# A semaphore for each buffer of turned blocks, two V tiles behind each of two score tiles, and three transposes on VectorE and through DRAM

## The reference

```python
h = film(rmsnorm(x, norm1_w), cond, film1_w, film1_b)   # x*(1+scale)+shift, scale and shift from cond
Q, K, V = h @ q_w + q_b, h @ k_w + k_b, h @ v_w + v_b
attn = softmax(einsum('bnd,bmd->bnm', Q, K) * D ** -0.5)
x = x + (einsum('bnm,bmd->bnd', attn, V) @ proj_w + proj_b)
h = film(rmsnorm(x, norm2_w), cond, film2_w, film2_b)
out = x + gelu(h @ mlp_w1 + mlp_b1) @ mlp_w2 + mlp_b2   # 256 -> 1024 -> 256
```

## Time and profile before

| | us |
|---|---|
| median of 3 runs | 234.42 (234.26 to 234.46) |
| profiled execution | 234.09 |
| its span | 232.2 |
| TensorE matmuls busy | 218.7 (94% of the span) |
| VectorE busy | 148.5 (64%) |
| ScalarE busy | 110.4 (48%) |
| GpSimd busy | 70.9 (31%) |

### The profile page before, as it was taken

How to read it: one execution, slowest core, us unless ns; L and a number is a source line. 1 busy time by engine, 2 the same in 40 slices (tenths; PEclk the granted TensorE clock), 3 DMA queues, 4 the chain that set the end, 5 groups by cost and what they waited for, 6 DMA issues and landing times.

```text
span 232.2 us, 3530 instructions
## 1 busy us (share of the span) xinstructions
PE 218.7 (94%) x1284; PEld 190.4 (82%) x1284; DVE 148.5 (64%) x288; ACT 110.4 (48%) x207; POOL 70.9 (31%) x102
## 2 busy tenths in 40 slices
PE   0998999999889999999999899999999999999994
PEld 0767988978768999998999799888888888888994
DVE  0599767669598998989989575143724372436223
ACT  3158654425333355333363881377437743744440
POOL 1575752002325512852543224321232123200000
PEclk9999999999999999999999999999999999999999
DMA  6994000054568968654556420000200020002002
GB/s 165 342 401 181 3 12 35 3 180 139 182 220 271 259 204 265 204 181 164 182 201 236 143 57 0 3 0 0 90 3 0 0 90 3 0 0 92 3 0 90
DMA packets 15713, 26.72 MB, mean 115 GB/s; under 512 B 1872, under 2 KB 10064, under 8 KB 15568
## 3 DMA queue, kind: packets, MB, share of 16 engines
q1 hardware_dynamic: 13392, 18.11, 24.9%
q10 hardware_dynamic: 2304, 8.39, 9.4%
HBM read 16.00 MB, written 10.49 MB: 114 GB/s over the span
## 4 chain that ended last, share of the span: by engine, by line
PE 78%; DVE 9%; DMA 7%; issue 2%; SPq 2%; ACT 1%; ACTq 0%; DVEq 0%
PE psum L711 36%; PE psum L785 16%; PE psum L836 8%; PE psum L828 5%; PE psum L834 5%; DMA raw<-in_film_wT_dram 3%; PE psum L729 3%; DMA crossing<-raw 2%; PE psum L703 2%; PE psum L723 2%; DVE hT L516 1%; DMA keys_first<-crossing 1%; ACT probsT L404 1%; PE psum L833 1%; SPq L190 1%
## 5 line engine op out<-in xcount | busy, mean ns | idle before, releaser
L658 DVE TENSOR_TENSOR G_all<-probs,G_all 128x512 fp32r<-128x512 f32 x32 | 22.4, 706 | 46.3 <-ACT G_all L453 46.3
L785 PEld LDWEIGHTS psum<-V_all,probsT 128*128 128x128 f32 x384 | 47.1, 189 | 5.4 <-DVE probsT L613 4.6
L785 PE MATMUL psum<-V_all,probsT 128*128 128x256 f32 x384 | 48.3, 283 | 2.7 <-DVE probsT L613 2.6
L711 PE MATMUL psum<-hT,w 128*128 128x512 f32 x192 | 49.1, 393 | 0.0
L711 PE MATMUL psum<-hT,G_all 128*128 128x512 f32 x192 | 46.5, 393 | 0.1
L453 ACT ACTIVATE probs<-psum,vcol 128x512 f32<-128x512 f32 x32 | 22.0, 689 | 44.5 <-PE psum L711 44.4
L711 PEld LDWEIGHTS psum<-hT,G_all 128*128 128x128 f32 x192 | 35.1, 188 | 7.5 <-ACT probs L393 0.6
L711 PEld LDWEIGHTS psum<-hT,w 128*128 128x128 f32 x192 | 35.5, 188 | 6.6
L404 ACT CAST probsT<-keys_first 128x1024 fp32r<-128x1024 f32 x16 | 16.8, 1050 | 42.8 <-DMA keys_first<-crossing 16.8
L312 POOL TENSOR_TENSOR x_rows<-x_rows,add_row 128x256 f32<-128x256 f32 x16 | 11.8, 739 | 69.2 <-DVE probsT L613 69.2
L836 PE MATMUL psum<-w,G_all 128*128 128x512 f32 x84 | 30.4, 396 | 0.0
(11 more groups left out here) (70 smaller groups left out, 258.4 us busy)
## 6 DMA issues: line engine op xcount, KB each, us to landing
keys_first<-crossing SPq DMA_DIRECT2D x64, 128.0 KB, 3.0
crossing<-turned ACTq DMA_DIRECT2D x8, 512.0 KB, 4.1
crossing<-raw ACTq DMA_DIRECT2D x8, 512.0 KB, 3.5
out_dram<-x_rows SPq DMA_DIRECT2D x8, 256.0 KB, 2.0
x_rows<-in_x_dram SPq DMA_DIRECT2D x3, 512.0 KB, 9.8
raw<-in_film_wT_dram SPq DMA_DIRECT2D x2, 512.0 KB, 8.7
raw<-in_mlp_w_dram SPq DMA_DIRECT2D x1, 1024.0 KB, 7.9
raw<-in_mlp_w_dram SPq DMA_DIRECT2D x4, 256.0 KB, 4.9
```

Of the source, the lines that this page charges most:

```text
L658: dve.tensor_tensor(gelu[:, m, LO, :], gelu_full[:, m % 2, :], gelu[:, m, HI, :].bitcast(F32), ALU.subtract).then_inc(gelu_ready, 1)
L711: last = pe.matmul(dst, stationary(a, k), moving(b, k), start=(n == len(tiles) * len(PASSES) - 1), stop=(n == 0))
L785: last = pe.matmul(bank(6 + t % 2, D), probsT[:, t % 2, a, k, :], V_all[:, t // KT * KT + k, s, :], start=(n == 0), stop=(n == KT * len(PA ...
```

## The change

The change has three parts.

1. `turned_out` becomes two semaphores, one for each buffer. A store no longer waits for the one before; what reuses a buffer waits for the store from that buffer.
2. `project_v` of group 3 no longer follows `scores(0)` as a whole. Its tiles 0 and 1 come behind `scores(1)`, tiles 2 and 3 behind `scores(2)`. The orders of ScalarE and VectorE in the first four tiles follow: `turn_blocks(t)` now comes ahead of `row_maximum(t + 1)`, `store_turned(0)` comes right behind `exp(0)`, and stores 2 and 3 stand on either side of `exp(3)`.
3. The second norm of groups 1 to 3 loses its transposes on TensorE. VectorE turns blocks of 32x32 of the normed rows (`turn_rows`), SP stores them to a DRAM tensor `rows_crossing` and loads them back with four DMAs (`cross_rows`), and `columns_after` reads them from SBUF. `normed_rows` and `turn_rows` of group `g + 1` stand behind `gelu_low(g, 0)` and ahead of `finished_rows(g - 1)`; for group 1 they stand behind `gelu_low(0, 2)` and ahead of `crossed_lo(15)`. The squares move one place ahead (group 1: behind `exp(15)`; others: behind GELU 6 of two groups before), and `inverse_rms` of group 1 moves into GpSimd's attention loop, at tile 13. SP's stores of finished rows are interleaved with `cross_rows` and written out without a loop.

```diff
+        rows_crossing = nc.dram_tensor("rows_crossing", [GROUPS, P, GT * D], F32)
+        turned_rows = raw[:, 0:GT * D]
+        columns_first = raw[:, GT * D:2 * GT * D].rearrange("p (a d j n) -> p a d j n", a=QT, d=DT, j=GT)
...
-        turned_out = sem("turned_out")
+        turned_out = [sem("turned_out_even"), sem("turned_out_odd")]
...
-                sp.wait_ge(turned_out, 16 * (t + 1))
+                sp.wait_ge(turned_out[t % 2], 16 * (t // 2 + 1))
...
+            def cross_rows(g):
+                sp.wait_ge(rows_turned, g)
+                sp.dma_start(rows_crossing[g, :, :], turned_rows).then_inc(rows_out, 16)
+                sp.wait_ge(rows_out, 16 * g)
+                sp.wait_ge(h_done, DT * (GROUPS + g))
+                for q in range(QT):
+                    sp.dma_start(
+                        columns_first[q * Q:(q + 1) * Q, :, :, :, :].rearrange("p a d j n -> p a (d j n)"),
+                        rows_crossing[g, :, q * GT * DT * Q:(q + 1) * GT * DT * Q].rearrange("(a p) n -> p a n", p=Q),
+                    ).then_inc(columns_in, 16)
...
+            cross_rows(1)
+            cross_rows(2)
+            store_rows(0)
+            cross_rows(3)
+            for g in range(1, GROUPS):
+                store_rows(g)
...
+                if t == 13:
+                    inverse_rms(GROUPS + 1)
...
-                if t >= 1:
-                    act.wait_ge(turned_out, 16 * t)
-                act.dma_start(crossing[t, :, :], turned[t % 2]).then_inc(turned_out, 16)
+                act.dma_start(crossing[t, :, :], turned[t % 2]).then_inc(turned_out[t % 2], 16)
...
+                    act.wait_ge(columns_in, 16 * QT * g)
+                    for d in range(DT):
+                        act.activation(h_full[:, d, :].rearrange("p (j a n) -> p j a n", j=GT, a=QT),
+                                       columns_first[:, :, d, :, :].rearrange("p a j n -> p j a n"), ACT.Identity,
+                                       bias=coef[:, 1, g // 2, DT + d:DT + d + 1],
+                                       scale=coef[:, 1, g // 2, d:d + 1]).then_inc(h_done, 1)
...
-            high_V(GROUPS - 1, range(2))
             for t in range(TILES):
-                if t == 1 or t > LAG:
+                if t > LAG:
                     store_turned(t - 1)
                 if t >= LAG - 1:
                     crossed_hi(t - LAG + 1)
+                if 2 <= t < LAG:
+                    store_turned(t - 1)
+                if t in (1, 2):
+                    high_V(GROUPS - 1, range(2 * t - 2, 2 * t))
                 exp(t)
-                if t == 0:
-                    high_V(GROUPS - 1, range(2, GT))
-                if 2 <= t <= LAG:
-                    store_turned(t - 1)
+                if t in (0, LAG - 1):
+                    store_turned(t)
...
+            squares_after(1)
             store_turned(TILES - 1)
...
+                    if m == 5 and g + 1 < GROUPS:
                         columns_after(g + 1)
+                    if m == 6 and g + 2 < GROUPS:
+                        squares_after(g + 2)
...
+            def turn_rows(g):
+                dve.wait_ge(xn_done, TILES + GT * (g + 1))
+                dve.wait_ge(mlp_ready, 8)
+                if g > 1:
+                    dve.wait_ge(rows_out, 16 * (g - 1))
+                dve.transpose(turned_rows.rearrange("p (q d j n) -> p d j q n", q=QT, d=DT, j=GT),
+                              xn[:, :, :].rearrange("p j (d q n) -> p d j q n", d=DT, q=QT)).then_inc(rows_turned, 1)
...
             for t in range(TILES):
+                if 2 <= t < LAG:
+                    turn_blocks(t - 1)
                 row_maximum(t)
                 if t == 0:
-                    low_V(GROUPS - 1, range(2))
                     turn_blocks(0)
-                    low_V(GROUPS - 1, range(2, GT))
+                if t in (1, 2):
+                    low_V(GROUPS - 1, range(2 * t - 2, 2 * t))
+                if t == 2:
                     group_terms(GROUPS - 1)
                 if t >= LAG - 1:
                     crossed_lo(t - LAG + 1)
-                if 2 <= t <= LAG:
-                    turn_blocks(t - 1)
+                if t == LAG - 1:
+                    turn_blocks(t)
...
             gelu_low(0, 2)
+            normed_rows(GROUPS + 1, GT)
+            turn_rows(1)
             crossed_lo(TILES - 1)
...
                     gelu_low(g, m)
-                    if before and m == 0:
+                    if m == 0 and g + 1 < GROUPS:
+                        normed_rows(g + (GROUPS + 1), g * GT + GT)
+                        turn_rows(g + 1)
+                    if m == 0:
                         finished_rows(g - 1)
...
             scores(1)
-            for t in range(2, TILES):
+            project_v(GROUPS - 1, range(2))
+            scores(2)
+            project_v(GROUPS - 1, range(2, GT))
+            for t in range(3, TILES):
...
-                    if more and m == 4:
-                        transpose_rows(g + (GROUPS + 1))
```

More of the change, by code:

```diff
@@ L230, in _, with store_rows @@
                     ).then_inc(keys_in[t % 2], 16)
[L232 to L236, removed]
+            def cross_rows(g):
[8 more added lines that the diff above has]
+                    ).then_inc(columns_in, 16)
+            def store_rows(g):
+                b, first = divmod(g * GT, KT)
+                for j in range(0, GT, 2):
+                    sp.wait_ge(rows_done, TILES + g * GT + j + 2)
+                    sp.dma_start(out_v[:, b, first + j:first + j + 2, :],
+                                 x_rows[:, g * GT + j:g * GT + j + 2, :]).then_inc(stored, 16)
+            cross_rows(1)
[4 more added lines that the diff above has]
+                store_rows(g)
             sp.wait_ge(stored, 16 * TILES // 2)
@@ L442, in _ @@
                 if t == TILES - 2:
-                    columns_after(0, 4)
+                    columns_after(0)
             def gelu_tile(g, m, before):
@@ L463, in _, with mlp @@
             gelu_tile(0, 3, False)
[L464 to L471, removed]
+            def mlp(g):
+                for m in range(0 if g else EARLY, HT):
+                    gelu_tile(g, m, g > 0)
+                    if m == 5 and g + 1 < GROUPS:
                         columns_after(g + 1)
+                    if m == 6 and g + 2 < GROUPS:
+                        squares_after(g + 2)
             for g in range(GROUPS):
-                mlp(g, g > 0, g < GROUPS - 1)
+                mlp(g)
         @block.vector
@@ L669, in _ @@
             add_attention(TILES - 1)
-            normed_rows(GROUPS + 1, GT)
             def finished_rows(g):
@@ L680, in finished_rows, with mlp @@
                     dve.tensor_tensor(row, bank(4 + j, D), row, ALU.add).then_inc(rows_done, 1)
[L682 to L683 removed]
+            def mlp(g):
+                for m in range(0 if g else EARLY, HT):
                     gelu_low(g, m)
[L685 removed]
+                    if m == 0 and g + 1 < GROUPS:
+                        normed_rows(g + (GROUPS + 1), g * GT + GT)
+                        turn_rows(g + 1)
+                    if m == 0:
                         finished_rows(g - 1)
[L687 to L690 removed]
+                    if m == 6 and g + 1 < GROUPS:
+                        low_columns(g + (GROUPS + 1), slice(g * GW + GW, g * GW + 2 * GW))
             for g in range(GROUPS):
[L693 removed]
+                mlp(g)
             finished_rows(GROUPS - 1)
@@ L731, in project_g, with project_v @@
                     last.then_inc(G_done, 1)
-            def project_v(g):
-                for j in range(GT):
+            def project_v(g, tiles=range(GT)):
+                for j in tiles:
                     if g > 0:
```

29 lines of the change are left out of this document (16 added, 13 removed).

## The result

| | before | after |
|---|---|---|
| median, us | 234.46 (9 runs, 234.07 to 235.34) | 233.67 (9 runs, 232.88 to 234.63) |
| profiled execution, us | 234.09 | 233.46 |
| its span, us | 232.2 | 231.6 |

What follows compares the result with a forecast made beforehand. The prediction took TensorE to bound the kernel (78% of the chain that ended last). Its terms, -1.99 - 2.61 + 1.46 + 2.14 = -1.00 us, took the profiled 234.09 to 233.09, a median of 233.4; range 232.0 to 235.4.

Steps and rivals of the forecast that it cites:

- Part 1, -1.99: Start of attention: semaphores and moved V tiles make attention(2) start at 67.85 instead of 69.84, 1.99 us gained.
- The loop of VectorE and ScalarE: First four tiles: row maximum, bias, exponential and block transpose repeat every 3.97 us, independent of TensorE.
- the crossing of tile 0: Start of attention: store 2.64 us, loads 4.60, crossed_hi(0) able to start at 53.31, cover 0.98 us.
- Transposes, -2.61: Second norm of groups 1 to 3: eight transposes each leave TensorE, 3 x 0.87 = 2.61 us gained.
- `attention(15)`, +1.46: End of attention: normed_rows and turn_rows(1) ahead of crossed_lo(15) make TensorE wait, 1.46 us lost.
- Row or rule on the transposes: Second norm: moving transposes gains 2.61 and loses 3.60 us; keeping them on TensorE by the skill's rule would give 232.4.
- Change of groups, +2.14: Hidden layer, changes to groups 1 and 2: finished_rows starts 1.07 us later each time, 2.14 lost; none at group 3.
- Hidden work: Second norm: DRAM round trips of 7.24 us and squares behind GELU 6 are covered, costing nothing.
- The sum: Whole kernel: gains and losses add to -1.00 us, giving a median of 233.4.
- The first (the VectorE work reaches no one): End of attention and group changes: new VectorE work delays nobody, -4.60 us, 229.8; chance 0.10.
- The second (tile 1's keys late): Start of attention: crossings collide, tile 1's keys land after 59.91 and TensorE waits, up to 235.4; chance 0.17.
- The third (the loop stays the pace): Past attention(0): VectorE and ScalarE still set the pace, attention(1) or (2) waits about 1.0 more, 234.4; chance 0.17.

Runs made afterwards that it cites:

- Store 1 later: Changed kernel with store 1 issued behind exp(2) on ScalarE, 2.6 us later, away from the loads of tile 0; 233.66 us, ratio 0.9965.
- part 1 alone: Kernel before with only the two semaphores and the new order of the first four tiles, transposes left on TensorE; 232.27 us, ratio 0.9905.
- both places mended: Changed kernel, crossed_lo(15) first and group 1's normed_rows and turn_rows each before an addition; groups 2 and 3's behind the previous group's last gelu_low; 229.56 us.

## Why the prediction was right, point by point

- **The views and what bounds.** The chain of waits and the two stretches picked from it were the ones in which the time moved; the starts between the rows of the table move with them, within 0.1.
- **Part 1, -1.99: mis-sized in this trace.** The loop of VectorE and ScalarE was right (3.97, 3.94, 3.94), and so was "no further wait" behind `attention(0)`. The term that failed is the crossing of tile 0, for which the text took the old 2.64 and 4.60 and so a cover of 0.98. It took 3.20 and 5.45, landed at 54.67 instead of 53.31, and the cover was gone: `attention(0)` at 57.03 instead of 56.61. The prediction had seen that store 1 would run beside these loads, and charged this to the store (4.31) alone; the loads pay as well. Store 1 later shows that share, 1.05 us of the loads. Of the store's own 0.56, about 0.2 goes with the instruction fetch and the rest is not explained. How much is lost changes from execution to execution: in the three traces with the same collision and a store of 2.97 or 2.98 before loads of 5.24 to 5.27, `attention(2)` comes 28.90 to 28.92 behind `scores(0)`, a gain of 1.9, nearly the predicted one.
- **Transposes, -2.61:** -0.88, -0.86, -0.81 in the three groups, -2.55.
- **`attention(15)`, +1.46:** 1.48 by its start, and 1.62 by `hidden(0,4)`. Most of the rest is that the tile behind a wait takes longer itself (below).
- **Row or rule on the transposes.** By the rule of the Trainium skill ("VectorE: DVE Perf Modes", section "Rules for kernel authors") the sum would have been part 1 alone, 232.4, and part 1 alone measured 232.27. As for this change, keeping to the rule was the better choice by 1.2 to 1.4 us. With both places mended the kernel with the transposes on VectorE is 2.7 us faster than that (229.56), so here the place decided, not the engine.
- **Change of groups, +2.14:** +1.05 and +1.07, none at group 3. `turn_rows`, which no row of before showed, took 1.25 and 1.17 to the next start, against the 1.16 taken.
- **Hidden work.** ScalarE's columns run at 150.44 with no wait for the crossed rows, 1.52 from SBUF against 1.45 from PSUM, and TensorE had no wait behind the squares. Both were rightly costed at nothing.
- **The sum.** -1.60 + 1.62 - 2.55 + 2.12 gives -0.41 to the last rows, -0.39 by the table; the stores' issue adds -0.2, which the sum didn't have, and the profiled execution is 0.63 faster. That the timed 0.98 meets the predicted 1.00 more closely than the trace does is chance: its interval is 0.6 to 1.4.
- **The rivals.** The first (the VectorE work reaches no one) is false of this change and, in its mechanism, true of the two better places. The second (tile 1's keys late) did not come: they landed at 59.23, 0.28 behind the predicted 58.95 and within the cover. The collision came one tile sooner, at tile 0, where with the longer store it made `attention(0)` 0.4 later. The third (the loop stays the pace) is refuted by the two rows without a bracket.

## What to carry to other kernels

Work taken off the engine that bounds is worth what it costs there less what it delays in its new queue: here 2.6 us of transposes gave a loss of 0.9 in one place and their full gain in another. So read who stands behind the new instruction on its engine, and behind that one too, since a swap only hands the wait to the next. A good place is a pause of the engine that the trace shows, not merely behind the work that is known to be urgent. When a transfer is brought forward, add its overlap to both transfers, the one that moves and the one it meets.

## What the runs showed of the hardware that was not expected

- A store of 512 KB issued 0.5 to 1.0 us behind the first of four loads of 128 KB made them take 5.24 to 5.51 in all, where with the store 2.05 and 2.36 behind they took 4.40 and 4.41.
- Two kinds of VectorE's work took longer beside GpSimd's additions: four normed rows 1.62 instead of 1.14, `gelu_low` about 1.0 instead of 0.69. The transposes (1.24 to 1.25) and the additions that read PSUM (0.42) took the same beside them.
- An attention tile that starts behind a wait takes 0.1 longer to the next start: 139.16 to 142.11 is 2.95 and 57.03 to 59.97 is 2.94, where 2.84 is usual. Here a wait on TensorE cost slightly more than its length.
